# Split Gram product: seven of eight blocks in high and low parts, with the copies on ScalarE and GpSimd

## What is computed

```python
x = x + 0.5 * ffn(layernorm(x))        # time mixing with the token before, sigmoid gate r, relu(k)^2, W_v
x = x + attention(layernorm(x))        # 16 heads of 16
x = x + 0.5 * ffn(layernorm(x))        # the same weights again

# attention, no softmax over tokens:
q = relu(x Wq^T) / 4 ; k = relu(x Wk^T) / 4 ; v = x Wv^T ; u = silu(x Wu^T)
kv  = sum over tokens of k (x) v       # one 16x16 matrix per head
out = norm(q kv) * u ;  out = out Wo^T
```

## Time and profile before

| | us |
|---|---|
| median of 3 runs | 328.40 (328.38 to 328.44) |
| profiled execution | 328.15 |
| span of its trace, first to last instruction | 326.3 |
| TensorE busy | 317.1 (97%) |
| VectorE busy | 236.2 (72%) |
| ScalarE busy | 226.3 (69%) |
| GpSimd busy | 167.2 (51%) |
| granted TensorE clock, mean | 1.000 |

### The profile page before, as it was taken

One profiled execution on the slowest core, in us unless ns is written; L12 is line 12 of the kernel. 1 busy time (PEld: TensorE's weight loads), 2 busy tenths in 40 slices (PEclk: granted clock), 3 DMA queues, 4 the chain that ended last, 5 costly groups with the idle time before them and its releaser, 6 DMA issues. The chain is left out here.

```text
span 326.3 us, 5493 instructions
## 1 busy us (share of the span) xinstructions
PE 317.1 (97%) x1932; PEld 282.9 (87%) x1932; DVE 236.2 (72%) x560; ACT 226.3 (69%) x443; POOL 167.2 (51%) x195
## 2 busy tenths in 40 slices
PE   6898999999999999999999999999999999999996
PEld 6676898889889988988988998989999999989885
DVE  3689984594665736865774688475979999989744
ACT  3699957848839558569239346459797969588861
POOL 4297855625438238246227016015285959585560
DMA  7960000000000000000000000000001020111103
GB/s 228 349 198 0 3 1 0 2 0 2 0 1 3 0 0 2 0 2 0 0 3 1 2 0 0 2 0 2 1 2 64 2 66 0 66 65 64 50 18 129
DMA packets 11035, 10.83 MB, mean 33 GB/s; under 512 B 768, under 2 KB 11008, under 8 KB 11008
## 3 DMA queue, kind: packets, MB, share of 16 engines
q1 hardware_dynamic: 10432, 10.23, 9.6%
q10 hardware_dynamic: 576, 0.26, 0.3%
HBM read 6.29 MB, written 4.19 MB: 32 GB/s over the span
## 5 line engine op out<-in xcount | busy, mean ns | idle before, releaser
L727 DVE SCALAR_TENSOR_TENSOR mix<-psA,mu,mix 128x512 f32<-128x512 f32 x64 | 44.1, 744 | 13.2 <-ACT mix L472 13.0
L336 POOL TENSOR_TENSOR mix_k_lo<-mix,mix_k_hi 128x512 fp32r<-128x512 f32 x30 | 39.5, 1335 | 13.3 <-ACT mix_k_hi L490 13.3
L472 ACT ACTIVATE mix<-psA,one_mu 128x511 f32<-128x511 f32 x64 | 39.5, 697 | 2.0 <-PE psA L1004 2.0
L987 PE MATMUL psRV<-ffn_hi,mix_r_hi 128*128 128x256 f32 x128 | 36.4, 284 | 0.0
L989 PE MATMUL psRV<-ffn_hi,mix_r_lo 128*128 128x256 f32 x128 | 35.7, 279 | 0.0
L988 PE MATMUL psRV<-ffn_lo,mix_r_hi 128*128 128x256 f32 x128 | 35.7, 279 | 0.0
L459 ACT ACTIVATE xn<-xs,shiftA,rstdA 128x256 f32<-128x256 f32 x59 | 30.8, 605 | 1.8 <-POOL shiftA L320 1.8
L747 DVE TENSOR_TENSOR mix_r_lo<-mix,mix_r_hi 128x512 fp32r<-128x512 f32 x30 | 27.5, 956 | 4.9 <-ACT mix_r_hi L490 4.9
L549 ACT ACTIVATE q_store<-psX 128x512 f32<-128x512 f32 x16 | 9.6, 598 | 29.2 <-PE psX L989 29.2
L1155 PE MATMUL psX<-wo,g_t 128*128 128x256 f32 x128 | 28.9, 379 | 0.0
L1100 PE MATMUL psK<-k_tok,xs 128*128 128x256 f32 x128 | 28.9, 379 | 0.0
(11 more groups left out here) (140 smaller groups left out, 905.8 us busy)
## 6 DMA issues: line engine op xcount, KB each, us to landing
xs<-x_dram SPq DMA_DIRECT2D x7, 512.0 KB, 8.7
out_dram<-xs SPq DMA_DIRECT2D x7, 512.0 KB, 2.9
out_dram<-xs SPq DMA_DIRECT2D x4, 128.0 KB, 1.7
xs<-x_dram ACTq DMA_DIRECT2D x2, 128.0 KB, 3.0
xs<-x_dram SPq DMA_DIRECT2D x2, 128.0 KB, 2.8
silu_u<-w_ffn_k_dram SPq DMA_DIRECT2D x1, 256.0 KB, 4.9
silu_u<-w_k_dram SPq DMA_DIRECT2D x1, 256.0 KB, 5.2
silu_u<-w_ffn_r_dram SPq DMA_DIRECT2D x1, 256.0 KB, 6.4
```

Source lines behind the costliest of these rows:

```text
L336: nc.gpsimd.tensor_tensor(mix_k_lo[:, h, :], mix[:, 0, h, :], mix_k_hi[:, h, :].bitcast(F32), ALU.subtract).then_inc(s_lo_k, 1)
L472: nc.scalar.activation(mix[:, rk, h, 1:BLOCK], psA[:, h, 0:BLOCK - 1], ACT.Copy, scale=one_mu[:, rk, h:h + 1]).then_inc(s_prev, 1)
L727: nc.vector.scalar_tensor_tensor(out=m, in0=psA[:, h, :], scalar=mu[:, rk, h:h + 1], in1=m, op0=ALU.mult, op1=ALU.add).then_inc(s_mix, 1)
L987: nc.tensor.matmul(dst, a_hi, b_hi, start=start, stop=False)
```

## The change

The Gram product of blocks 1 to 7 uses split operands. ScalarE writes `x1_hi` (one activation of 128x1024 for a block, after gram of the block before is done) and `k_hi` (two activations of 128x512); GpSimd subtracts to get `x1_lo` and `k_lo` (two instructions of 128x512 each). Block 0 keeps the fp32 form. To make room, `silu_u` and `q_store` hold six blocks and are used in turn, and the raw attention weights are loaded into `q_store`. In the stretches of blocks 6 and 7 some instructions change places.

```diff
+HELD = 6
-        silu_u = sb("silu_u", [P, NB * ROW])
-        q_store = sb("q_store", [P, NB, HALVES, BLOCK])
+        silu_u = sb("silu_u", [P, HELD * ROW])
+        q_store = sb("q_store", [P, HELD * HALVES * BLOCK])
-        raw_att = silu_u[:, 6 * ROW:6 * ROW + 3 * HALVES * D].rearrange(...)
+        raw_att = q_store[:, 4 * ROW:4 * ROW + 3 * HALVES * D].rearrange(...)
...
+            def x1_low(a):                                   # GpSimd
+                for g in range(2):
+                    pool.wait_ge(s_x1hi, a)
+                    nc.gpsimd.tensor_tensor(x1_lo[:, g * BANK:(g + 1) * BANK], row(xs, a, g * BANK, BANK),
+                                            x1_hi[:, g * BANK:(g + 1) * BANK].bitcast(F32),
+                                            ALU.subtract).then_inc(s_x1lo, 1)
+            def kt_low(a):
+                for g in range(2):
+                    pool.wait_ge(s_kt_hi, 2 * (a - 1) + g + 1)
+                    tiles = slice(2 * g, 2 * g + 2)
+                    nc.gpsimd.tensor_tensor(k_lo[:, tiles, :], k_tok[:, tiles, :], k_hi[:, tiles, :].bitcast(F32),
+                                            ALU.subtract).then_inc(s_kt_lo, 1)
...
-            for i in range(1, 5):
+            for i in range(1, 6):
                 act_low(i)
                 k_low(i + 1)
+                if i > 1:
+                    kt_low(i - 1)
                 scales_a(i + 2)
                 scales_b(i)
-            act_low(5)
-            k_low(6)
-            scales_a(7)
-            scales_b(5)
+                x1_low(i)
             norm_second(0)
             act_low(6)
             k_low(7)
+            kt_low(5)
             scales_b(6)
+            x1_low(6)
             scales_a(8)
             norm_second(1)
             act_low(7)
+            kt_low(6)
             scales_b(7)
             scales_a(9)
             norm_second(2)
+            x1_low(7)
+            kt_low(7)
             k_low(8)
...
+            def x1_high(a):                                  # ScalarE
+                act.wait_ge(s_x1, 2 * (a + 1))
+                act.wait_ge(s_gt, a)
+                nc.scalar.activation(x1_hi[:], row(xs, a), ACT.Identity).then_inc(s_x1hi, 1)
+            def kt_high(a, g):
+                act.wait_ge(s_kt, 4 * a + 2 * g + 2)
+                tiles = slice(2 * g, 2 * g + 2)
+                nc.scalar.activation(k_hi[:, tiles, :], k_tok[:, tiles, :], ACT.Identity).then_inc(s_kt_hi, 1)
...
-                for t in range(1, TILES):
-                    sigmoid_u(i - 1, t)
+                sigmoid_u(i - 1, 1)
+                if i > 1:
+                    kt_high(i - 1, 0)
+                sigmoid_u(i - 1, 2)
+                sigmoid_u(i - 1, 3)
+                if i > 1:
+                    kt_high(i - 1, 1)
                 mix_high(i + 1, 1)
...
                     square_heads(i - 5)
+                x1_high(i)
                 relu_q(i - 1)
...
             x2_high(7)
             previous(8)
+            x1_high(7)
             mix_high(8, 0)
             sigmoid_u(7, 0)
             sigmoid_u(7, 1)
-            mix_high(8, 1)
+            kt_high(7, 0)
             sigmoid_u(7, 2)
             sigmoid_u(7, 3)
+            kt_high(7, 1)
             keep_g_rows(2)
+            mix_high(8, 1)
             square_heads(3)
...
             projections(7)                                   # VectorE
+            gate_heads(3)
             r_low(8)
-            gate_heads(3)
...
                 pe.wait_ge(s_silu, 4 * a + 3)                # TensorE, gram(a)
+                if a > 0:
+                    pe.wait_ge(s_x1lo, 2 * a)
                 for f in range(HALVES):
                     for t in range(TILES):
...
+                        if f == 0 and t % 2 == 0:
+                            pe.wait_ge(s_kt_lo, 2 * (a - 1) + t // 2 + 1)
+                        rows = slice(t * D + f * P, t * D + (f + 1) * P)
+                        last = product(dst, x1_hi[:, rows], x1_lo[:, rows], k_hi[:, t, :], k_lo[:, t, :],
+                                       t == 0, t == TILES - 1)
```

More of the change, by code:

```diff
@@ L53, in macaron @@
         xs = sb("xs", [P, NB * ROW])
-        silu_u = sb("silu_u", [P, NB * ROW])
-        q_store = sb("q_store", [P, NB, HALVES, BLOCK])
+        silu_u = sb("silu_u", [P, HELD * ROW])
+        q_store = sb("q_store", [P, HELD * HALVES * BLOCK])
         raw_ffn = silu_u[:, 4 * ROW:4 * ROW + 2 * HALVES * D].rearrange("p (n c e) -> p n c e", n=2, c=HALVES)
-        raw_att = silu_u[:, 6 * ROW:6 * ROW + 3 * HALVES * D].rearrange("p (n c e) -> p n c e", n=3, c=HALVES)
+        raw_att = q_store[:, 4 * ROW:4 * ROW + 3 * HALVES * D].rearrange("p (n c e) -> p n c e", n=3, c=HALVES)
         wv = sb("wv", [P, HALVES, D])
@@ L100, in macaron @@
         k_tok = sb("k_tok", [P, TILES, D])
+        k_hi = sb("k_hi", [P, TILES, D], F32R)
+        k_lo = sb("k_lo", [P, TILES, D], F32R)
+        x1_hi = sb("x1_hi", [P, ROW], F32R)
+        x1_lo = sb("x1_lo", [P, ROW], F32R)
         g_acc = sb("g_acc", [P, HALVES, D])
@@ L165, in macaron @@
         s_kt = sem("s_kt")
+        s_kt_hi = sem("s_kt_hi")
+        s_kt_lo = sem("s_kt_lo")
+        s_x1hi = sem("s_x1hi")
+        s_x1lo = sem("s_x1lo")
         s_sig = sem("s_sig")
@@ L200, in tile_row, with q_half @@
             return row(tile, block, t * D, D)
+        def q_half(a, m):
+            return row(q_store, a % HELD, m * BLOCK, BLOCK)
         def added(n):
@@ L542, in sigmoid_u @@
                             act.wait_ge(done, 1)
-                nc.scalar.activation(tile_row(silu_u, a, t), (psX, psK)[t // 2][:, t % 2, D:2 * D], ACT.Sigmoid,
+                nc.scalar.activation(tile_row(silu_u, a % HELD, t), (psX, psK)[t // 2][:, t % 2, D:2 * D], ACT.Sigmoid,
                                      scale=rstdB[:, a, t:t + 1]).then_inc(s_sig, 1)
@@ L548, in relu_q @@
                     act.wait_ge(s_q, 2 * a + m + 1)
-                    nc.scalar.activation(q_store[:, a, m, :], psX[:, m, :], ACT.Relu).then_inc(s_relu_q, 1)
+                    nc.scalar.activation(q_half(a, m), psX[:, m, :], ACT.Relu).then_inc(s_relu_q, 1)
             def square_heads(j):
@@ L624, in _ @@
             sigmoid_r(7, 1)
-            for t in range(1, TILES):
-                sigmoid_u(6, t)
+            sigmoid_u(6, 1)
+            kt_high(6, 0)
+            sigmoid_u(6, 2)
+            sigmoid_u(6, 3)
+            kt_high(6, 1)
             keep_g_rows(1)
@@ L769, in silu @@
                 dve.wait_ge(s_sig, 4 * a + t + 1)
-                su = tile_row(silu_u, a, t)
+                su = tile_row(silu_u, a % HELD, t)
                 nc.vector.scalar_tensor_tensor(out=su, in0=(psX, psK)[t // 2][:, t % 2, D:2 * D],
@@ L800, in gate_heads @@
                     nc.vector.tensor_tensor(gout[:, 2 * g:2 * g + 2, :].rearrange("p t d -> p (t d)"), ps[:, g, :],
-                                            row(silu_u, j, g * BANK, BANK), ALU.mult).then_inc(s_gu, 1)
+                                            row(silu_u, j % HELD, g * BANK, BANK), ALU.mult).then_inc(s_gu, 1)
             def head_norms(j):
@@ L1095, in gram @@
                 pe.wait_ge(s_silu, 4 * a + 3)
+                if a > 0:
+                    pe.wait_ge(s_x1lo, 2 * a)
                 for f in range(HALVES):
                     for t in range(TILES):
[L1098 to L1101, removed]
+                        dst = psK[:, 0, f * D:(f + 1) * D]
+                        if a == 0:
+                            if f == 0:
+                                pe.wait_ge(s_kt, t + 1)
+                            last = nc.tensor.matmul(dst, row(xs, 0, t * D + f * P, P), k_tok[:, t, :],
+                                                    start=(t == 0), stop=(t == TILES - 1))
+                            continue
+                        if f == 0 and t % 2 == 0:
[3 more added lines that the diff above has]
+                                       t == 0, t == TILES - 1)
                 last.then_inc(s_gt, 1)
@@ L1133, in attend @@
                         last = nc.tensor.matmul(ps[:, t // 2, (t % 2) * D + h * P:(t % 2) * D + (h + 1) * P],
-                                                q_store[:, j, h, tok(t)], kv_bd[:, j // BB, h, :],
+                                                q_half(j, h)[:, tok(t)], kv_bd[:, j // BB, h, :],
                                                 start=True, stop=True)
```

## The result

| | before | changed |
|---|---|---|
| median, us | 328.39 (328.1 to 328.44) | 324.45 (324.05 to 325.01) |
| profiled execution, us | 328.15 | 324.32 |
| span of its trace, us | 326.3 | 322.5 |

The ratio is 0.9883, 95% interval 0.9866 to 0.9900: 3.9 us faster, and 1.4 us faster than forecast. A second comparison (e0_again) gave 0.9893 (0.9879 to 0.9907). The direction and the main terms of the sum were right. The time lies just inside the lower end of the range, 324.4 to 327.5, and nearer to the first rival's 324.15 than to the forecast's 325.9.

A forecast was written before the change was run, and what follows sets the result against it. TensorE, busy in 317.1 of 326.3 us, was taken to bound the kernel. The sum was 328.15 - 4.25 + 0.6 + 0.2 + 1.0 = 325.7 us, 325.9 in the median's terms; range 324.4 to 327.5.

The forecast's parts named there:

- first rival: Whole kernel: TensorE gives 4.25 us and nothing waits, 324.15 us; chance 0.17.
- TensorE's work: Gram and neighbouring runs of blocks 1 to 7: split matmuls save 4.25 us, bounds 3.0 to 4.6.
- ffn_k(3), ffn_k(4), kv(0) wait for keep_g: After blocks 1 to 3: TensorE waits 0.2 us each for VectorE's keep_g, 0.6 us in all.
- project_out(0) waits for g_t: Block 5's stretch: kt_high(5,1) in front delays keep_g_rows(0) on ScalarE, so project_out(0) starts 0.2 us late.
- gram(7) waits for k_lo: Block 7: kt_low's second half ends at 207.05, needed at 206.2; wait 1.0 us, bounds 0.6 and 1.6.
- The step that was mis-sized: VectorE in block 2's stretch: keep_g ends 0.64 us later, at 94.0 for 93.38, past ffn_k's new start of 93.89.
- The lock: Shared port pair: VectorE's first residual add and GpSimd's kt_low shut each other out; 0.6 us in the sum.
- k_lo late in the early blocks: Blocks 1 to 4: k_lo lands at 89.6 for 88.98, at worst 327.9 us, likelier 326.9; chance 0.18.
- GpSimd becomes the pace: kt_low's second half in all seven blocks: each waits like block 7, 332.0 us; chance 0.06, including a loss by GpSimd.
- All of it is gained: Whole kernel: TensorE's saving of 4.25 us is kept and nothing waits, 324.15 us; chance 0.17.
- all bad ends at once: Upper bound of the forecast: 3.6 us saved and waits of 1.5, 0.4 and 1.6 give 328.3 us.

The follow-up runs named there:

- e0_again: The changed kernel run once more with nothing edited, against the kernel before: median 324.53 us, ratio 0.9893.
- e1: The kernel before with gram of blocks 1 to 7 as split matmuls on weight tiles lying ready, no copies made: 323.75 us, ratio 0.9872.
- e4: The changed kernel with keep_g(1) to keep_g(3) ahead of r_low on VectorE and keep_g_rows(0) ahead of mix_high on ScalarE: 324.30 us, ratio 0.9892.
- e8: The changed kernel with one more VectorE add of 128x512 in front of keep_g(1), keep_g(2) and keep_g(3): 326.75 us, ratio 0.9964.
- e3: The changed kernel with gram(7) reordered, both feature halves of tiles 0 and 1 first, then of tiles 2 and 3: 324.00 us, ratio 0.9880.
- e2: The changed kernel with gram in fp32 as before, all high and low copies made but not read: 327.84 us, ratio 0.9998 to before.
- e6_gram7_plain: The changed kernel with gram(7) back in fp32 and its high and low copies left out: 324.69 us, ratio 0.9900.

## Why the forecast was right, and where it was off

| step of the forecast | forecast, us | measured |
|---|---|---|
| TensorE's work | -4.25 | -4.00 (e1) |
| ffn_k(3), ffn_k(4), kv(0) wait for keep_g | +0.6 | +0.20 and +0.04 in the two traces by single rows, nothing in the totals against e4; margin 0.14 by e8 |
| project_out(0) waits for g_t | +0.2 | 0 (starts at 154.56, g_t written by 154.43) |
| gram(7) waits for k_lo | +1.0 | +0.83 in the stretch (against e1), +0.79 in gram(7) itself; 0.70 regained by e3 |
| sum, ffn_k(0) to ffn_k(8) | -2.45 | -3.36 and -3.10 |
| up to ffn_k(0) | 0 | -0.47 and -1.03, scatter |

*The bound.* TensorE's time passed on: with only TensorE's work changed (e1), ffn_k(0) to ffn_k(8) got 4.00 us shorter, the differences of the gram runs and the runs beside them in the timeline add up to the same, and the median fell by 4.2.

*The size of the saving.* Blocks 1 to 3 gave 0.57 to 0.59 each for 0.64 (a split gram takes 2.86 and not 2.83), blocks 4 and 5 0.58 for 0.56 and 0.55, blocks 6 and 7 together 1.11 for 1.22.

*The step that was mis-sized:* "With 0.64 more (the end of kt_low at 88.4 less 87.78) it ends at 94.0." The lock was there; what it costs was less. I let VectorE's add begin only when GpSimd had ended and then take its full 0.69. Measured, it takes 1.15 where a full wait of 0.60 and a full 0.69 would be 1.29, and keep_g comes 0.37 late, not 0.64. Besides the 0.14, 0.09 of the delay fell into time in which VectorE had waited for TensorE anyway. By the Trainium skill (SBUF — State Buffer, section SBUF: two separate sides) the loser of this port pair blocks fully until the other instruction is done. The trace agrees in the main: alone the add takes 0.69, and here it ends 0.55 behind the subtract (87.75 and 87.20), so all but 0.14 of its own time lies behind it. As 5.48 lies below 5.67, most of the 0.6 us did not come. Since the margin is 0.14, and less where ffn_v takes its shorter time, the reasoning was right about what is late next, and 0.3 us wrong about when (0.1 behind the start of ffn_k forecast, 0.19 ahead of it measured).

*The other small step:* "157.5 plus release and weight load, 0.2 late". A release costs 0.05 (e8: 94.30 to 94.35) and the run starts behind it; g_t was in time by 0.13.

*Block 7* went as the chain was worked out: x1_low where k_low stood, k_lo's second part behind kt_high(7,1), 0.17 less than 1.0. The two relevant distances were 1.46 us from gram(7)'s start to k_lo's second part (202.04 to 203.50; forecast 1.55) and 0.8 to the matmul that needs it (forecast 0.7). The rival "k_lo late in the early blocks" falls: k_lo's second part is written at 87.20, and gram wants it at 87.80. "GpSimd becomes the pace" falls with e2. "All of it is gained" was, to within 0.2 us, the state of six blocks of seven.

*Where luck comes in:* the waits were priced 0.8 to 0.9 us too high and the saving 0.25 too high; the two errors partly cancel. With 324.45 against a lower end of 324.4, and a scatter of 0.5 us in the start alone, it was partly chance that the time fell inside the range and not outside. The range itself was not built as the text says: its upper sum takes 3.6 us for the saving where the stated lower bound is 3.0, so "all bad ends at once" would be 328.9 and not 328.3.

*What no step held:* 0.47 us of the first comparison lies before ffn_k(0). It belongs to no edit. A lower median from there would have been taken for a gain of the change, had the stretches not been compared one by one.

## What to carry to other kernels

Where one engine is busy all the time, price the saved work on it, then ask for each result that it consumes how much margin is left once the work has gone: here 1.15 us became 0.14 and stayed nearly free, and a chain with no slack (block 7) cost 0.83. When only part of an operand comes late, order the matmuls so that the late part is used last: e3 changed no work and took back 0.70 of the 0.83. And compare traces stretch by stretch, between marks that both kernels have, when the effect is near the scatter of whole runs.

## What the runs showed of the hardware

- VectorE's add with two SBUF inputs, met by a GpSimd subtract with 0.60 us to go, took 0.46 us longer. A gate instruction with one operand in PSUM, beside the same subtract in the changed kernel (85.88 to 86.57, the subtract from 85.90), kept its 0.69.
- The dummy transposes at the start begin at about 5 a microsecond (0.20 us apart) and later at about 9 (0.11 apart). The moment of the change is not fixed: it lies between 5.6 (e0_again) and 8.6 us (e6_gram7_plain) in the eleven traces. The counts below are higher because they include matmuls that reach over an edge. Stretches of before and of e0_again (start and end, length, PE busy and count, granted clock, DMA):

```profile
6.00:7.00 1.00, 1.00 (x7) 1.00 1.09 381
7.00:8.00 1.00, 1.00 (x8) 1.00 1.08 373
8.00:9.00 1.00, 1.00 (x11) 1.00 1.10 355
```

```profile
5.00:6.00 1.00, 1.00 (x8) 1.00 1.04 242
6.00:7.00 1.00, 1.00 (x11) 1.00 1.01 329
7.00:8.00 1.00, 1.00 (x12) 1.00 1.05 307
```

The granted clock in these rows is 1.00 throughout, 2.4 GHz, also where the pace is about half; the count shows what that column does not. From the first start to the last end the 40 took 7.0 us in the trace of before and 6.0 in that of e0_again.

- A run of matmuls that had to wait starts slower: ffn_k takes 2.92 us behind a wait and 2.80 without, kv(0) 0.89 and 0.81 (e8_keepg_late and e4_early).
